# Second cross attention of a four-layer gated kernel: output projection, update and residual add for pairs of batches

## The reference

```python
q = ln @ Wq
kv_input = jnp.concatenate([xn, ln], axis=-2)
k, v = jnp.split(kv_input @ Wkv, 2, axis=-1)
q, k, v = (to_heads(q) * scale, to_heads(k), to_heads(v))      # 8 heads of 64
attn = softmax(einsum('bhid,bhjd->bhij', q, k))
out = einsum('bhij,bhjd->bhid', attn, v)                        # back to 8 * 64 = 512 features
return out @ Wout                                              # 512 -> 128
...
x = x + tanh(g_xattn[2]) * that
```

## Time and profile before

| what | value |
|---|---|
| median of three runs | 596.26 us (595.03 to 597.34) |
| profiled execution | 596.09 us |
| its span | 594.3 us |
| mean granted TensorE clock | 0.996 |
| loop of stage 4 | about 223 to 290 us of the span |

### The profile page before, as it was taken

One profiled execution on the slowest core, in us unless ns is written; L12 is line 12 of the kernel. 1 busy time (PEld: TensorE's weight loads), 2 busy tenths in 40 slices (PEclk: granted clock), 3 DMA queues, 4 the chain that ended last, 5 costly groups with the idle time before them and its releaser, 6 DMA issues.

```text
span 594.3 us, 10734 instructions
## 1 busy us (share of the span) xinstructions
PE 564.9 (95%) x3703; PEld 409.6 (69%) x3703; DVE 381.7 (64%) x736; ACT 387.9 (65%) x787; POOL 245.7 (41%) x231
## 2 busy tenths in 40 slices
PE   9999998999999997999899999999989999999997
PEld 6567766687665775776555556577768788888885
DVE  2678857556641657777354676478838666666665
ACT  4277877655666447888665656677875576666663
POOL 5006683486013100111015781000023788888884
PEclk9999999999999999999999999999999999999999
DMA  8300001161000000000000102000001666665740
GB/s 258 139 2 2 2 1 33 28 159 54 0 2 1 1 0 1 1 2 1 2 0 3 39 15 66 1 2 1 3 9 36 165 176 169 181 184 169 192 123 36
DMA packets 14852, 33.55 MB, mean 56 GB/s; under 512 B 2913, under 2 KB 8433, under 8 KB 14673
## 3 DMA queue, kind: packets, MB, share of 16 engines
q1 hardware_dynamic: 14800, 32.89, 19.4%
HBM read 32.03 MB, written 0.85 MB: 55 GB/s over the span
## 4 chain that ended last, share of the span: by engine, by line
PE 73%; DVE 9%; ACT 7%; issue 7%; POOL 3%; ACTq 0%; DVEq 0%; POOLq 0%
PE bank L842 9%; PE bank L844 8%; PE bank L843 8%; PE bank L726 5%; PE bank L737 4%; PE bank L752 3%; PE bank L685 3%; ACT wa L1408 2%; PE bank L700 2%; PE bank L648 2%; PE bank L1243 2%; PE bank L642 2%; PE bank L1118 2%; PE bank L1132 2%; PE bank L1107 1%
## 5 line engine op out<-in xcount | busy, mean ns | idle before, releaser
L502 POOL TENSOR_TENSOR h_lo<-wc,h_hi 128x512 fp32r<-128x512 f32 x56 | 72.6, 1300 | 15.2 <-ACT h_hi L1477 15.2
L842 PE MATMUL bank<-xn_hi,w_hi 128*128 128x512 f32 x168 | 66.0, 393 | 3.4 <-DVE xn_lo L1962 3.1
L844 PE MATMUL bank<-xn_hi,w_lo 128*128 128x512 f32 x168 | 65.4, 390 | 0.0
L843 PE MATMUL bank<-xn_lo,w_hi 128*128 128x512 f32 x168 | 65.4, 389 | 0.0
L1951 DVE TENSOR_TENSOR wb<-arena,bank 128x512 f32<-128x512 f32 x64 | 44.0, 687 | 32.9 <-PE bank L844 32.8
L1477 ACT ACTIVATE h_hi<-wc 128x512 fp32r<-128x512 f32 x56 | 35.3, 633 | 39.4 <-DVE wc L1959 29.8
L494 POOL TENSOR_TENSOR w_lo<-ring,w_hi 128x384 fp32r<-128x384 f32 x42 | 42.7, 1019 | 17.7 <-ACT w_hi L1454 17.7
L1739 DVE TENSOR_TENSOR wa<-bank,row_max 128x512 f32<-128x512 f32 x64 | 44.3, 692 | 7.5 <-ACT wb L1354 4.3
L1354 ACT ACTIVATE wb<-wa 128x512 f32<-128x512 f32 x64 | 40.1, 630 | 13.7 <-DVE wa L1739 13.3
L1735 DVE TENSOR_REDUCE row_max<-bank 128x4 f32<-128x512 f32 x64 | 43.6, 682 | 5.9 <-PE bank L726 5.4
L502 POOL TENSOR_TENSOR h_lo<-arena,h_hi 128x512 fp32r<-128x512 f32 x26 | 33.7, 1295 | 24.2 <-ACT h_hi L1477 24.2
(11 more groups left out here) (347 smaller groups left out, 1393.0 us busy)
## 6 DMA issues: line engine op xcount, KB each, us to landing
arena<-comb_rows SPq DMA_DIRECT2D x64, 256.0 KB, 4.1
ring<-in_experts SPq DMA_DIRECT2D x42, 192.0 KB, 2.5
ring<-in_experts SPq DMA_DIRECT2D x8, 256.0 KB, 3.2
mats<-in_mats SPq DMA_DIRECT2D x1, 1472.0 KB, 10.2
mats<-in_mats SPq DMA_DIRECT2D x1, 832.0 KB, 6.7
mats<-in_mats SPq DMA_DIRECT2D x2, 320.0 KB, 7.9
x<-in_x_t SPq DMA_DIRECT2D x1, 512.0 KB, 4.3
context<-in_ctx_t SPq DMA_DIRECT2D x1, 512.0 KB, 4.9
```

The costliest lines, as they stand in the source:

```text
L502: nc.gpsimd.tensor_tensor(h_lo[:, v % 3, :], hidden_of(v), h_hi[:, v % 3, :].bitcast(f32), ALU.subtract).then_inc(m_h_lo, 1)
L842: mm(out, w, x_, start=start, stop=False)
L843: mm(out, w, x_rest, start=False, stop=False)
L844: return mm(out, w_rest, x_, start=False, stop=stop)
```

## The change

`through_o2`, `update2` and GpSimd's add run once for two batches. `copy_o2` writes its batch into one half of a buffer for a pair, `o_pair`, a view of `sq` as [128, 4 groups, 256 columns]. When b is even, `through_o2` and `update2` do nothing. When b is odd, `through_o2` makes four products of 256 columns, `update2` scales 256 columns, and GpSimd adds 256 columns. The stage then makes four updates and not eight, so PER_STAGE[4] is 4. GpSimd's hardware loop is written out as four instructions with constant addresses. Nothing else moves: TensorE's and ScalarE's order stays, with the steps of the even batches absent.

```diff
+        o_pair = sq[:, :, :].rearrange("p c t -> p (c t)").rearrange("p (g t) -> p g t", g=4)
-        PER_STAGE = [8, 2, 2, 2, 8, 2, 8, 2]
+        PER_STAGE = [8, 2, 2, 2, 4, 2, 8, 2]
...
-            with pool.Fori(0, B) as b:
-                pool.wait_ge(update_ready, u_count(4) + b + 1)
-                xs = x[:, :, :].rearrange("p c t -> p (c t)")
-                dst = xs[:, ds(b * P, P)]
-                nc.gpsimd.tensor_tensor(dst, dst, upd[:, 0:P], ALU.add).then_inc(x_updated, 1)
+            for k in range(B // 2):
+                pool.wait_ge(update_ready, u_count(4) + k + 1)
+                dst = x[:, k // 2, 256 * (k % 2):256 * (k % 2) + 256]
+                nc.gpsimd.tensor_tensor(dst, dst, upd[:, 0:256], ALU.add).then_inc(x_updated, 1)
...
             def through_o2(b):
+                if b % 2 == 0:
+                    return
                 pe.wait_ge(l_ofm, b + 1)
-                pe.wait_ge(update_ready, u_count(4) + b)
+                pe.wait_ge(update_ready, u_count(4) + b // 2)
                 for g in range(4):
-                    last = mm(bank[7][:, 0:P], w[:, (12 + g) * P:(13 + g) * P], o_fm[:, g, :],
+                    last = mm(bank[7][:, 0:256], w[:, (12 + g) * P:(13 + g) * P], o_pair[:, g, :],
                               start=(g == 0), stop=(g == 3))
                 last.then_inc(l_y, 1)
...
                 def copy_o2(b):
                     act.wait_ge(l_pv, 2 * b + 2)
-                    if b > 0:
-                        act.wait_ge(l_y, b)
-                    fn(o_fm[:, :, :], bank[6][:, :].rearrange("p (g t) -> p g t", g=4), ACT.Copy).then_inc(l_ofm, 1)
+                    if b >= 2:
+                        act.wait_ge(l_y, b // 2)
+                    fn(o_pair[:, :, b % 2 * P:b % 2 * P + P], bank[6][:, :].rearrange("p (g t) -> p g t", g=4), ACT.Copy).then_inc(l_ofm, 1)
 
                 def update2(b):
-                    act.wait_ge(l_y, b + 1)
-                    update(4, bank[7][:, 0:P], 14 + b, P)
+                    if b % 2 == 0:
+                        return
+                    act.wait_ge(l_y, b // 2 + 1)
+                    update(4, bank[7][:, 0:256], 14 + b // 2, 256)
...
-            units(UNITS, 6, 24, SCALE_A, B, B)
+            units(UNITS, 6, x_count(5, 1), SCALE_A, B, B)
```

## The result

The changed kernel takes 599.88 us in the median of 22 runs (597.68 to 602.63), the kernel before 596.98 us in 22 runs beside them. The ratio is 1.005, with a 95% interval of 1.0038 to 1.0063: slower by 2.3 to 3.8 us. The plain difference of the medians can be up to 1 us away from it. The predicted time was 598.6, the range 596.0 to 600.4. The measurement lies on the border between "within 0.5%" and "slower by over 0.5%", and the forecast had put three quarters of the chance on the near side, most of the rest beyond it. A second comparison, in another session, gave 1.0038 (1.0017 to 1.0059).

The account below looks back on a forecast made before the run. The prediction took a chain alternating between TensorE, ScalarE and VectorE to bound the loop, with TensorE's queue only 0.08 us earlier. +1.74 us in the loop and +0.66 behind it made +2.40, so 598.6 us, range 596.0 to 600.4.

Parts of the forecast that it names:

- Thin passes gain nothing: In the loop passes without through_o2, T2 still waits for VectorE's normalised probabilities: gain 0.
- Wide records of 256 columns at 0.215 us: On TensorE, each record of the wide through_o2 takes 0.215 us, so eight take 1.72 us.
- The floor of 0.133: Lower bound in us for a 256-column record on TensorE, if weight loads set the pace; loop term then 0.
- T2 late by 0.58 us in three passes: In the loop, the wide through_o2 delays T2 in the passes of b = 2, 4, 6: +1.74 us.
- The room of 0.08 us: Before T2 in the loop, TensorE's queue is only 0.08 us earlier than the chain; upper bound 0.28.
- eight narrow records at 0.1325 us: In the loop, the eight 128-column records of the old through_o2 take 1.06 us of streaming on TensorE.
- with 0.28 us of room: Bound for the loop's term if TensorE has 0.28 us of room before T2: +1.14 us.
- rival B: Wide products cost little inside the loop, through more room before T2 or closer spacing: middle 597.2 us; chance 0.13.
- The end: Behind the loop, the last through_o2 is in the chain and becomes 0.66 us longer.
- Rival A: TensorE's throughput bounds the loop, so the kernel gains 1.6 us, to 594.7; chance 0.05.
- ScalarE, GpSimd, copy with a stride: In the loop and behind it, merged update, merged add and strided copy_o2 change the time by 0.
- Rival C: TensorE's clock falls in thinned loop passes, 600.0 us for one fall; chance 0.07, with the later fall spared 0.05.

Follow-up runs that it names:

- e4: Kernel before with two more products of 128 columns, never read, ahead of through_o2 in each of the seven passes; ratio 1.0026, +1.6 us.
- e5: Changed kernel's merged update and add, but TensorE keeps eight groups of products of 128 columns; ratio 0.9999 against the kernel before.
- e6: The changed kernel measured again, same code, in another session; ratio 1.0038 against the kernel before.
- e3: Changed kernel with each wide group split, two products in each of two passes, the last pair's four together behind the loop; ratio 1.0011, +0.7 us against the kernel before.
- e2: Kernel before with only the last pair, batches 6 and 7, made wide; batches 0 to 5 singly; ratio 1.0013, +0.8 us.

## Why the prediction was right, and where only by luck

**Thin passes gain nothing: right.** T2 waits 0.98 us there. Three of the four are 0.06 us shorter than before, by the weight load that e4 shows hidden, not by the missing group: the fourth, T2(0) to T2(1), lacks a group too and is 7.75 us. I had claimed exactly no payback.

**Wide records of 256 columns at 0.215 us: right.** 0.216 us. The floor of 0.133 didn't apply. Its reason, that weight loads set the pace at 128 columns, didn't hold either: 0.111 us at 128 columns is little more than half of 0.216.

**T2 late by 0.58 us in three passes: right in its place.** 8.33 us was forecast and came, to 0.01. With the 0.06 given back three times, the loop's term is +1.58 in place of +1.74.

**The room of 0.08 us, and eight narrow records at 0.1325 us: wrong.** The step that failed is "Its eight records take 1.06 us of streaming". That is the group's busy time, whose last record runs to its modelled end, 0.275 us after its start. The spacing is 0.111 us (e4), the streaming 0.89 us and the room 0.25 us. The loader's idle 0.28 us was the nearer reading, and I had set it aside. The forecast of 8.33 us didn't suffer, since it used T2's distance of 1.14 us directly and only the wide group's length. For the same reason the bound "with 0.28 us of room" was wrong, and rival B with it as far as it rests on the room: a wide group overruns by 1.73 − 1.14 us whatever the narrow one took. The room came out at 0.25 us, and the loop still cost +1.58.

**The end: the term was mis-sized by it.** 1.72 − 1.06 = 0.66 was the estimate, 0.83 came (1.73 − 0.89). Sum: +1.58 + 0.83 = +2.41 against +2.40. The two errors, −0.16 and +0.17, cancelled; that the sum came out to 0.01 is luck.

**Rival A was priced too high.** With 0.111 us for 128 columns and 0.216 for 256, eight narrow groups take 8 × 0.89 = 7.1 us and four wide ones 4 × 1.73 = 6.9. There was hardly any TensorE work to save: narrow records follow each other nearly as fast as their columns stream. Even if TensorE had bound the loop, the gain would have been 0.2 us and not 1.6.

**ScalarE, GpSimd, copy with a stride: right,** all at 0 in the loop and at its end (e5). The k rows products cover the add behind the loop, as said.

**Rival C, a clock fall in thin passes: did not happen.** The clock was 1.00 in the passes, 6.52 us of records in 7.68. In front of the loop and behind it the clock falls in some executions and not in others of the same code (changed kernel and e6), so the little work in front of 294 us, which the prediction names, doesn't settle it.

**The time.** 596.26 + 2.4 was said; 596.98 + 2.9 came. Of the 2.9 us, 2.41 are placed. As 2.41 lies inside the interval (2.3 to 3.8), the times don't show that there is more. Executions that show the same mean clock can be compared with each other. Six values of the clock occur with both kernels, over the 93 executions of before and 34 of the changed kernel whose clock is on record. At 0.994 the medians are 597.15 (23) and 599.44 (4), +2.3 us; at 0.991 they are 598.18 (40) and 600.51 (6), +2.3 us. The other four, with 2 to 4 executions in the smaller group, give +1.5, +1.5, +1.6 and +2.8. A straight line in the clock through all 127, with one step for the change, puts the step at +2.2 us, give or take 0.2. The changed kernel's mean clock is a little lower (0.9925 against 0.9930 over all of them). Whether the change moves the moments at which the clock falls, or whether that is chance, stays open. The chance of "slower by over 0.5%", 0.24, was low for a forecast of +0.4% with this scatter.

## What to carry to other kernels

Before merging products, look at the distance between their starts at both widths. Here it was 0.111 us at 128 columns and 0.216 at 256, so the streaming of the columns set the pace and merging had almost nothing to save. In a software pipeline an even load matters more than a small one: a piece of work beside the chain is free up to the room in front of the next waiting step, here 1.14 us for the whole group, and doubling it in every second pass costs the overrun while the empty pass gives nothing back. The same wide products, two a pass, cost nothing. Read streaming time from where the next thing starts when it isn't waiting, not from the busy time of a group, which includes the last one's end.

## What the runs showed that I had not expected

A group of transposes that had to wait loads its first weights uncovered, 0.05 us of the pass (0.58 us from T2 to PV0 against 0.53). GpSimd's add took longer when it began early in VectorE's division (`normalise`). The 256 columns took 0.74 us in the changed kernel's loop, 1.07 in those of e3 and e5, and 0.72 behind the loop, away from it. First the changed kernel, then e5:

```profile
246.93 0.69 DVE L1797 TENSOR_TENSOR wb<-wa,sum 128x512 f32<-128x512 f32 x1
247.47 0.74 POOL L588 TENSOR_TENSOR x<-x,upd 128x256 f32<-128x256 f32 x1 [45.20 <-ACT upd L1349]
```

```profile
249.34 0.69 DVE L1796 TENSOR_TENSOR wb<-wa,sum 128x512 f32<-128x512 f32 x1
249.54 1.07 POOL L588 TENSOR_TENSOR x<-x,upd 128x256 f32<-128x256 f32 x1 [44.90 <-ACT upd L1348]
```

128 columns go the same way: 0.90 us in e2's loop, begun 0.11 us after the start of the division, 0.79 in the loop of before, begun 0.21 us after it, and 0.45 behind the loop. e2 has constant addresses and before has one from a register, so the register isn't what made them slow. That the division holds the add back fits all of these, but no run was made to isolate it. And one core's executions of the same program differ by up to 6 us (597.13 to 603.21 in e6), nearly in step with the mean clock that they show, 0.999 to 0.986.
